# The neighbouring batches' work put inside the second stage's searches, and the next batch's normalisation between the products of the fourth and sixth stage

## Chip, core and metric

The kernel runs on one core of one Trainium2 chip. TensorE (PE) multiplies matrices, VectorE (DVE), ScalarE (ACT) and GpSimd (POOL) work element by element, SyncE (SP) issues the DMAs. The metric is the device time of one execution in microseconds (us).

## The reference

Eight layers run one after the other on x, a residual stream of 4 batches x 512 rows x 512 columns; each begins with a layer norm of x. What matters here are three of them:

```python
# second stage (L0_ffn): 2048 hidden values a row, of which the largest 204 are kept
z = x_flat @ ternary_quant(W_syn).T + b_syn
k = max(1, int(N * (1.0 - TARGET_SPARSITY)))
topv, _ = jax.lax.top_k(z, k)
hidden = jnp.where(z >= topv[:, -1:], jax.nn.relu(z), 0.0)
out = hidden @ ternary_quant(W_out).T + b_out
return layernorm(x + out, gamma, beta)
# fourth stage (L1_ffn)
out = jnp.einsum('bsi,oi->bso', x, weight * scale_weight[:, None]) + bias
# sixth stage (L2_ffn): 8 gates a row, the best one's low-rank update is applied
gate = sigmoid(imp_slope * (score - imp_center)); sel_scale = gate.max(axis=1); sel_idx = gate.argmax(axis=1)
return (1.0 - sel_scale) * x + sel_scale * mod_x_bias
```

## The kernel before, in words

The code writes one program for each engine by hand, and semaphores alone order them; within an engine the order is that of the code. There are eight stages, A to H, and all engines meet at the end of each (`end_stage`). x stays on chip in `X` as 16 tiles of 128 rows. A batch is four tiles. Float32 operands of products are split into a high and a low part (`xT_hi`, `xT_lo`), the high part copied by ScalarE and the low part subtracted by VectorE out of the same PSUM bank.

**Second stage.** Per batch, in a loop: `norm_vector`, `norm_pool`, `norm_tensor` and `norm_scalar` normalise and transpose four tiles; TensorE makes z in `ps` (32 products a tile) and VectorE writes it to `b_z` (L1142). VectorE takes the maximum of each of the four tiles' rows (L1151). Then a search of 26 rounds finds each row's threshold by halving: in a round each tile (here also called a group, 0 to 3) has its values above a candidate counted; groups 0 and 1 are counted by VectorE (`search_vector`, L158), 2 and 3 by ScalarE with a Sign (`search_scalar`, L166), and GpSimd makes the next candidate from each count in the order 2, 0, 3, 1 (`search_pool`, L185 to L190, and L191, which quarters the step once a round). A group's next count waits for its candidate (`search_try`), GpSimd waits for its count (`search_cnt`). After the search VectorE masks z (L1158), TensorE transposes the hidden values (L1784), ScalarE and VectorE split them (L759, L1165), TensorE multiplies by the second matrix (32 products a tile), and VectorE adds the rest, normalises and adds to `X` (L1174 to L1186).

**Fourth stage.** Per batch: normalise four tiles, then for each tile 12 products and one update of `X` (L1281).

**Sixth stage.** Per batch: normalise four tiles, 12 products of 136 columns a tile (L1410 takes them out of PSUM), the gates in some 35 small operations around an exponential on ScalarE, a transposition of the chosen gates, and the output product with its update of `X` (L1450, L1452).

## Time and profile before

| | |
|---|---|
| median of three runs | 3627.24 us (3622.87 to 3627.38) |
| the profiled execution | 3632.95 us |
| its span, first to last instruction | 3631.2 us |
| mean granted TensorE clock | 0.814 of full speed |
| second stage | 159.9 to 1072.1 us of the span |
| fourth stage | 1297.9 to 1404.8 us |
| sixth stage | 2282.2 to 2443.4 us |

The page gives the busy time of each engine. A window gives the same for a stretch of the span, with the granted clock of TensorE (1.00 is 2.4 GHz, 0.50 is 1.2). A group of instructions is one source line on one engine; the idle time in its row is that of its engine just before it, with what ended it. The median and the profiled execution are 5.7 us apart.

### The profile page before, as it was taken

What the parts mean: (1) busy time and instruction counts of PE and PEld (TensorE: products, weight loads), DVE (VectorE), ACT (ScalarE), POOL (GpSimd) and SP (SyncE); (2) the same over time, 40 slices, a digit from 0 to 9 for tenths busy, and PEclk for the clock granted to TensorE, in tenths of its full rate; (3) what the DMA queues carried; (4) which work ended last, traced back from release to release, by engine and by line L of the source; (5) the groups of instructions that cost most, each with busy time, mean ns of one, the idle gap of its engine ahead of it and who ended that gap; (6) DMA issues with size and microseconds to landing.
All of it is one profiled execution on the core that took longest, in us unless ns stands there. A gap on an engine that the chain in (4) does not pass through costs nothing.

```text
span 3631.2 us, 41752 instructions
## 1 busy us (share of the span) xinstructions
PE 2379.0 (66%) x12378; PEld 1982.2 (55%) x12378; DVE 2470.6 (68%) x4232; ACT 1680.2 (46%) x3289; POOL 823.8 (23%) x2434
## 2 busy tenths in 40 slices
PE   3322505226051066699999999456999928999998
PEld 2212404114041055577878788445887827888887
DVE  7888697886979953276767777555777756454443
ACT  3466292561929801255555555114666614333332
POOL 1044161340614500022222222012223320000000
PEclk7665857658575586699999999657999969999999
DMA  4000000000000003644444443003222225332232
GB/s 166 12 0 0 0 0 0 0 0 0 0 13 0 0 18 127 237 138 129 137 129 137 122 146 98 8 12 85 58 56 59 53 76 180 104 111 96 99 111 73
DMA packets 93950, 253.40 MB, mean 70 GB/s; under 512 B 17692, under 2 KB 18972, under 8 KB 86628
## 3 DMA queue, kind: packets, MB, share of 16 engines
q1 hardware_dynamic: 91236, 243.00, 21.5%
q0 software_dynamic: 2560, 8.42, 0.6%
q8 instruction: 87, 1.43, 0.2%
q14 instruction: 67, 0.55, 0.0%
HBM read 162.20 MB, written 22.05 MB: 51 GB/s over the span
## 4 chain that ended last, share of the span: by engine, by line
PE 45%; DVE 11%; issue 9%; ACT 4%; DMA 2%; POOL 1%; SPq 1%; POOLq 0%; ACTq 0%; DVEq 0%; PEldq 0%
PE ps L87 12%; PE ps L89 11%; PE ps L88 11%; PE ps L1905 3%; DVE c_junks L1252 2%; PE ps L2041 1%; ACT c_junks L166 1%; DVE g_pT_lo L1521 1%; PE ps L1895 1%; PE ps L1896 1%; PE ps L1931 1%; PE ps L1934 1%; DVE e_k_lo L1309 1%; DVE e_cT_lo L1387 1%; ACT g_p L927 1%
## 5 line engine op out<-in xcount | busy, mean ns | idle before, releaser
L166 ACT ACTIVATE b_junk_high<-b_z,b_tk 128x2048 bf16<-128x2048 f32 x208 | 414.7, 1994 | 210.3 <-POOLq L172 149.9
L158 DVE TENSOR_SCALAR_CACHE_REDUCE b_junk_low<-b_z,b_tk 128x2048 bf16<-128x2048 f32 x208 | 471.8, 2342 | 1.7 <-POOLq L175 1.7
L1784 PE MATMUL ps<-ident,b_z 128*128 128x128 f32 x256 | 43.3, 341 | 560.1 <-DVEq L1159 533.5
L1784 PEld LDWEIGHTS ps<-ident,b_z 128*128 128x128 f32 x256 | 40.1, 182 | 564.1 <-DVEq L1159 535.2
L604 POOL TENSOR_SCALAR e_p<-e_p,e_st 128x512 f32<-128x512 f32 x256 | 173.6, 698 | 662.4 <-DVE e_st L1329 662.4
L826 ACT ACTIVATE e_p<-ps,e_st 128x512 f32<-128x512 f32 x256 | 173.8, 686 | 144.4 <-DVE e_st L1318 144.4
L1324 DVE TENSOR_TENSOR e_pT_lo<-ps,e_pT_hi 128x512 fp32r<-128x512 f32 x256 | 174.0, 680 | 46.2 <-ACT e_pT_hi L832 42.3
L638 POOL TENSOR_SCALAR g_p<-g_p,g_st 128x128 f32<-128x128 f32 (+3 forms) x256 | 132.2, 537 | 311.7 <-DVE g_st L1502 311.7
L185 POOL TENSOR_SCALAR b_tk<-b_tk 128x1 f32<-128x1 f32 x416 | 122.0, 293 | 299.0 <-DVEq L197 192.4
L927 ACT ACTIVATE g_p<-ps,g_st 128x128 f32<-128x128 f32 (+3 forms) x256 | 131.6, 526 | 80.7 <-DVE g_st L1497 80.7
L1613 DVE TENSOR_TENSOR h_h<-ps,h_sg 128x512 f32<-128x512 f32 (+1 forms) x80 | 50.9, 637 | 173.5 <-ACT h_sg L976 173.3
L1318 DVE TENSOR_REDUCE e_st<-ps 128x1 f32<-128x512 f32 x256 | 163.7, 681 | 2.3 <-PE ps L1896 2.3
L976 ACT ACTIVATE h_sg<-ps 128x512 f32<-128x512 f32 (+1 forms) x80 | 44.3, 553 | 246.0 <-PE ps L89 246.0
L166 ACT ACTIVATE c_junks<-c_sim,c_tk 128x512 bf16<-128x512 f32 x208 | 146.7, 707 | 1.0 <-POOL c_tk L190 1.0
L87 PE MATMUL ps<-xT_hi,h_w_hi 128*128 128x512 f32 (+1 forms) x384 | 139.1, 362 | 9.3 <-issue 6.9
L1521 DVE TENSOR_TENSOR g_pT_lo<-ps,g_pT_hi 128x512 fp32r<-128x512 f32 (+1 forms) x192 | 103.4, 594 | 54.3 <-ACT g_pT_hi L940 54.3
L832 ACT ACTIVATE e_pT_hi<-ps 128x512 fp32r<-128x512 f32 x256 | 138.7, 599 | 3.3 <-PE ps L1905 3.3
L1252 DVE TENSOR_SCALAR_CACHE_REDUCE c_junks<-c_sim,c_tk 128x512 bf16<-128x512 f32 x208 | 140.0, 745 | 0.0
L89 PE MATMUL ps<-xT_hi,h_w_lo 128*128 128x512 f32 (+1 forms) x384 | 137.2, 357 | 0.0
L1905 PE MATMUL ps<-ident,e_p 128*128 128x128 f32 x1024 | 134.3, 275 | 4.2 <-POOL e_p L604 2.3
L88 PE MATMUL ps<-xT_lo,h_w_hi 128*128 128x512 f32 (+1 forms) x384 | 136.7, 356 | 0.0
L1832 PE MATMUL ps<-c_a,ident 128*128 128x128 f32 x128 | 26.6, 292 | 164.1 <-DVE c_a L1212 164.1
(465 smaller groups left out, 8244.0 us busy)
## 6 DMA issues: line engine op xcount, KB each, us to landing
h_w<-in_l_blob SPq DMA_DIRECT2D x80, 512.0 KB, 3.6
e_g<-e_g_kept SPq DMA_DIRECT2D x32, 1024.0 KB, 6.1
e_qkw<-e_qkw_kept SPq DMA_DIRECT2D x32, 640.0 KB, 4.2
h_w<-in_l_blob SPq DMA_DIRECT2D x80, 256.0 KB
e_xs<-e_q_hi SPq DMA_DIRECT2D x128, 128.0 KB, 2.3
e_g_kept<-e_g SPq DMA_DIRECT2D x8, 1024.0 KB, 6.0
e_xs<-e_k_hi SPq DMA_DIRECT2D x64, 128.0 KB, 2.3
e_k<-e_k_hi SPq DMA_DIRECT2D x64, 128.0 KB, 2.3
```

The costliest lines, as they stand in the source:

```text
L87: pe.matmul(o, l_hi, r_hi, start=start, stop=False)
L88: pe.matmul(o, l_hi, r_lo, start=False, stop=False)
L89: return pe.matmul(o, l_lo, r_hi, start=False, stop=stop)
L158: dve.tensor_scalar(junk[j], data[:, j, :], cand[:, j:j + 1], 0.0, ALU.is_ge, ALU.add, accum_out=cnt[:, j:j + 1])\
L166: act.activation(junk[j], data[:, j, :], ACT.Sign, bias=cand[:, j:j + 1], accum_out=cnt[:, j:j + 1])\
L604: pool.tensor_scalar(p, p, e_st[:, h % 2, 8 + t:9 + t], 1.0, ALU.mult, ALU.mult).then_inc(sem("e_scaled"), 1)
L826: act.activation(e_p[:, h % 2, t, :], ps[:, (h * TB + t) % 3, :], ACT.Exp, bias=e_st[:, h % 2, t:t + 1], accum_out=e_st[:, h % 2, 4 + t:5 ...
L927: act.activation(g_p[:, n % 2, G_ROW[t]:G_ROW[t + 1]], ps[:, G_BANK[t], G_COL[t]:G_COL[t] + (t + 1) * P], ACT.Exp, bias=g_st[:, n % 2, t:t ...
L1252: dve.tensor_scalar(c_junk[j], c_sim[:, j, :], cand[:, j:j + 1], 0.0, ALU.is_ge, ALU.add, accum_out=cnt[:, j:j + 1])\
L1318: dve.tensor_reduce(e_st[:, h % 2, t:t + 1], ps[:, (h * TB + t) % 3, :], AX.X, ALU.max, negate=True)\
L1324: dve.tensor_tensor(e_pT_lo[:, c, :], ps[:, 3 + (h * TB + c) % 3, :], e_pT_hi[:, c, :].bitcast(F32), ALU.subtract)\
L1905: t = pe.transpose(ps[:, 3 + n % 3, t_ * P:(t_ + 1) * P], e_p[:, h % 2, t_, c * P:(c + 1) * P], ident[:, :])
```

## The change

In the second stage the loops are written out. While batch i is searched, the rounds are taken in pairs (p = 0 to 12) and the engines do pieces of two other batches between the counts: of batch i+1 the statistics, normalisation, transposes, z and maxima, at the pairs that the tables `B_XN`, `B_LOW`, `B_MADE`, `B_Z` and `B_TOP` name for its four tiles; of batch i-1 the mask, the hidden values' transposes and split, the second product, and the last normalisation. z is held twice (`b_z[:, 2, ...]`); the hidden values go through two 128-column slots of `xT_hi` and `xT_lo`, a quarter of a tile at a time. In odd rounds group 1 is counted by ScalarE instead of VectorE, with the sign turned and GpSimd's comparison with it. The counts' output is int8 instead of bf16. ScalarE normalises x (an Identity with scale and bias) instead of VectorE, and makes the rest for the second residual the same way; the tail has two fused operations where there were three. VectorE loads `b_out` into `xn[:, 3]` and it is waited for at the start. After the last search, batch 3's rest has nothing beside it.

In the fourth stage the 16 tiles go through one software pipeline: tile n's product is issued with tile n+2's transposes ahead of it and tile n+3's normalisation on VectorE, and the first tiles are normalised before the weights are waited for. In the sixth stage the next batch's statistics, normalisation and transposes are put between the gates and the outputs of this one (`f_xn` is held twice), and operations that were issued for each tile are issued once for four.

```diff
+B_XN, B_LOW, B_MADE, B_Z, B_TOP = (2, 4, 7, 8), (4, 6, 8, 9), (4, 7, 8, 9), (6, 8, 9, 10), (7, 10, 11, 11)
 # SyncE
+                sp.dma_start(b_out, inp["b_out"].partition_broadcast(P)).then_inc(sem("b_bsyn_in"), 16)
 # GpSimd, second stage
+                def b_round_pool(i, r):
+                    now, then = (odd, even) if r % 2 else (even, odd)
+                    for g in (2, 0, 3, 1):
+                        q = slice(g, g + 1)
+                        pool.wait_ge(sem(f"search_cnt{g}"), ROUNDS * i + r + 1)
+                        if g == 1 and r % 2:
+                            k(pool.tensor_scalar(take[:, q], cnt[:, q], float(HID - 2 * SYN_K), now[:, q], ALU.is_le, ALU.mult))
+                        else:
+                            enough = float(SYN_K if g < 2 else 2 * SYN_K - HID)
+                            k(pool.tensor_scalar(take[:, q], cnt[:, q], enough, now[:, q], ALU.is_ge, ALU.mult))
+                        k(pool.tensor_tensor(low[:, q], low[:, q], take[:, q], ALU.add))
+                        pool.tensor_tensor(cand[:, q], low[:, q], then[:, q], ALU.add).then_inc(sem(f"search_try{g}"), 1)
 # ScalarE, second stage
+                def b_hidden_scalar(i, j, q):
+                    n = (i * TB + j) * 4 + q
+                    act.wait_ge(sem("b_hT_ps"), n + 1)
+                    if n >= 2:
+                        act.wait_ge(sem("b_hT_used"), n - 1)
+                    act.activation(xT_hi[:, :, (2 + q % 2) * P:(3 + q % 2) * P], ps[:, q % 2, :].rearrange("p (c t) -> p c t", c=4), ACT.Copy)\
+                        .then_inc(sem("b_hT_hi"), 1)
+                def b_count_scalar(i, r, g):
+                    act.wait_ge(sem(f"search_try{g}"), search_tries(i, r))
+                    act.activation(b_junk[:, g, :], b_z[:, i % 2, g, :], ACT.Sign, bias=cand[:, g:g + 1], scale=-1.0 if g == 1 else 1.0,
+                                   accum_out=cnt[:, g:g + 1]).then_inc(sem(f"search_cnt{g}"), 1)
+                for i in range(B):
+                    for p in range(ROUNDS // 2):
+                        b_count_scalar(i, 2 * p, 2)
+                        b_count_scalar(i, 2 * p, 3)
+                        if i and p < 2 * TB:
+                            for q in range(2):
+                                b_hidden_scalar(i - 1, p // 2, p % 2 * 2 + q)
+                        if i and p in (2, 4, 6, 8):
+                            b_rest_scalar(i - 1, (p - 2) // 2)
+                        if i + 1 < B:
+                            for t in range(TB):
+                                if p == B_XN[t]:
+                                    b_xn_scalar(i + 1, t)
+                                if p == B_LOW[t]:
+                                    b_turned_scalar(i + 1, t)
+                        b_count_scalar(i, 2 * p + 1, 2)
+                        b_count_scalar(i, 2 * p + 1, 3)
+                        b_count_scalar(i, 2 * p + 1, 1)
 # VectorE, second stage
+                for i in range(B):
+                    for p in range(ROUNDS // 2):
+                        b_count_vector(i, 2 * p, 0)
+                        b_count_vector(i, 2 * p, 1)
+                        b_count_vector(i, 2 * p + 1, 0)
+                        if i:
+                            if p in (2, 4, 6, 8):
+                                b_sum_vector(i - 1, (p - 2) // 2)
+                            if p < 2 * TB:
+                                for q in range(2):
+                                    b_hidden_vector(i - 1, p // 2, p % 2 * 2 + q)
+                            if p in (1, 3, 5):
+                                b_mask_vector(i - 1, (p + 1) // 2)
+                            if p in (3, 5, 7, 9):
+                                b_tail_vector(i - 1, (p - 3) // 2)
...
+                    b_end_vector(i)
+                    if i + 1 < B:
+                        b_begin_vector(i + 1)
+                    b_mask_vector(i, 0)
 # TensorE, second stage
+                for i in range(B):
+                    for p in range(ROUNDS // 2):
+                        if i and p < 2 * TB:
+                            for q in range(2):
+                                b_hidden_tensor(i - 1, p // 2, p % 2 * 2 + q)
+                        if i + 1 < B:
+                            for t in range(TB):
+                                if p == B_LOW[t]:
+                                    b_turn_tensor(i + 1, t)
+                        if i and p < 2 * TB:
+                            for q in range(2):
+                                b_out_tensor(i - 1, p // 2, p % 2 * 2 + q)
+                        if i + 1 < B:
+                            for t in range(TB):
+                                if p == B_MADE[t]:
+                                    b_z_tensor(i + 1, t)
 # VectorE, fourth stage
+                for n in range(TILES):
+                    i, j = divmod(n, TB)
+                    if n + 3 < TILES:
+                        xn_vector("d", (n + 3) // TB, (n + 3) % TB)
+                    if j == 0 and i + 1 < B:
+                        dve.wait_ge(sem("ln_xn"), TB * (ln_turn("d", i) + 1))
+                        d_norm_vector(i + 1)
+                    k.later(dve.tensor_tensor(X[:, n, :], X[:, n, :], d_rows[:, 1, :], ALU.add))
+                    if n + 2 < TILES:
+                        d_turned_vector(n + 2)
+                    dve.wait_ge(sem("y_ps"), n + 1)
 # TensorE, sixth stage
+                for i in range(B):
+                    pe.wait_ge(sem("f_m"), i + 1)
...
+                    for u in range(2):
+                        if i + 1 < B:
+                            f_turn_tensor(i + 1, 2 * u)
+                            f_turn_tensor(i + 1, 2 * u + 1)
+                        f_y_tensor(i, 2 * u)
+                        f_y_tensor(i, 2 * u + 1)
+                    if i + 1 < B:
+                        for j in range(TB):
+                            f_a_tensor(i + 1, j)
```

Here is VectorE inside a search before: the loop body with both its counts (b_junk_low is the count's output, b_z the values, b_tk the candidates and counts).

```order
L1151 TENSOR_REDUCE b_tk<-b_z 128x1
L37 REGISTER_ALU
L1152 MEMSET b_tk 128x2
L1153 TENSOR_SCALAR b_tk<-b_tk 128x2
L37 REGISTER_ALU
L195 TENSOR_SCALAR b_tk<-b_tk 128x2
L196 TENSOR_TENSOR b_tk<-b_tk 128x2
L37 REGISTER_ALU
L154 UNCONDITIONAL_BRANCH
L154 ISA
L158 TENSOR_SCALAR b_junk_low,b_tk<-b_z,b_tk 128x2048 x2
L154 REGISTER_ALU
```

And VectorE in the second search of the changed kernel, pairs 5 and 6 (L1273 is the count, L1289 the hidden values' low part, L1284 the mask, L1305 to L1308 a tail, L1296 to L1301 a sum).

```order
L1273 TENSOR_SCALAR b_junk,b_tk<-b_z,b_tk 128x2048 x3
L1289 TENSOR_TENSOR xT_lo<-ps,xT_hi 128x4x128 x2
L1284 SCALAR_TENSOR_TENSOR b_z<-b_z,b_edge 128x2048
L1305 SCALAR_TENSOR_TENSOR xn<-xn,b_st,b_rows 128x512
L1307 SCALAR_TENSOR_TENSOR xn<-xn,b_st,b_rows 128x512
L1308 TENSOR_TENSOR X_rows<-X_rows,xn 128x512
L1273 TENSOR_SCALAR b_junk,b_tk<-b_z,b_tk 128x2048 x3
L1296 SCALAR_TENSOR_TENSOR xn<-ps,b_st,xn 128x512
L1298 TENSOR_TENSOR xn<-xn 128x512
L1299 BN_STATS b_st<-xn 128x6
L1300 BN_AGGR b_st<-b_st 128x2
L1301 TENSOR_SCALAR b_st<-b_st 128x1
```

Three counts a pair are left where there were four, and behind them stand the pieces of the neighbouring batches.

ScalarE before: a loop of two counts a round (L166), and the hidden values' copies (L759) behind the whole search.

```order
L162 ISA
L166 ACTIVATE b_junk_high,b_tk<-b_z,b_tk 128x2048 x2
L162 REGISTER_ALU
L162 COMPARE_AND_BRANCH
L758 ISA
L759 ACTIVATE b_hT_hi<-ps 128x512
L758 REGISTER_ALU
L759 ACTIVATE b_hT_hi<-ps 128x512
```

ScalarE in the second search of the changed kernel, pairs 1 to 4 (L814 is the count, L802 the hidden values' high part, L809 the rest, L789 the normalisation, L794 the normalised tile's high part).

```order
L814 ACTIVATE b_junk,b_tk<-b_z,b_tk 128x2048 x5
L802 ACTIVATE xT_hi<-ps 128x4x128 x2
L814 ACTIVATE b_junk,b_tk<-b_z,b_tk 128x2048 x5
L802 ACTIVATE xT_hi<-ps 128x4x128 x2
L809 ACTIVATE xn<-X_rows,b_ln 128x512
L789 ACTIVATE xn<-X_rows,b_ln 128x512
L814 ACTIVATE b_junk,b_tk<-b_z,b_tk 128x2048 x5
L802 ACTIVATE xT_hi<-ps 128x4x128 x2
L814 ACTIVATE b_junk,b_tk<-b_z,b_tk 128x2048 x5
L802 ACTIVATE xT_hi<-ps 128x4x128 x2
L809 ACTIVATE xn<-X_rows,b_ln 128x512
L794 ACTIVATE xT_hi<-ps 128x4x128
```

Five counts stand between two groups of pieces, where a search had four a pair and nothing between them.

## Rows read from the trace of the kernel before

**Rows 1.** The page's busy time of each engine, share of the span and instructions.

```profile
PE 2379.0 (66%) x12378; PEld 1982.2 (55%) x12378; DVE 2470.6 (68%) x4232; ACT 1680.2 (46%) x3289; POOL 823.8 (23%) x2434
```

**Rows 2.** Windows: length, busy us of each engine, clock, DMA share, GB/s.

```profile
206.90:331.70 124.80, 0.00 (x0) 0.00 (x0) 122.99 (x111) 106.20 (x104) 75.50 (x338) 0.50 0.00 0
331.70:388.10 56.40, 41.15 (x192) 34.55 (x192) 40.11 (x57) 8.92 (x16) 2.23 (x5) 0.80 0.00 0
...
159.90:1072.10 912.20, 299.00 (x1344) 246.84 (x1344) 751.63 (x825) 469.66 (x496) 315.01 (x1372) 0.66 0.00 1
...
1297.90:1404.80 106.90, 63.15 (x256) 50.94 (x256) 57.84 (x107) 11.37 (x17) 4.07 (x4) 0.79 0.04 15
...
2282.20:2443.40 161.20, 80.55 (x328) 67.66 (x328) 92.22 (x269) 25.11 (x58) 4.04 (x4) 0.54 0.02 5
```

**Rows 3.** Groups by line: count, busy us, mean ns, idle before.

```profile
L158 DVE TENSOR_SCALAR_CACHE_REDUCE b_junk_low<-b_z,b_tk 128x2048 bf16<-128x2048 f32 x208 | 471.8, 2342 | 1.7 <-POOLq L175 1.7
L166 ACT ACTIVATE b_junk_high<-b_z,b_tk 128x2048 bf16<-128x2048 f32 x208 | 414.7, 1994 | 210.3 <-POOLq L172 149.9 <-POOL b_tk L190 56.1
...
L1142 DVE SCALAR_TENSOR_TENSOR b_z<-ps,b_st,b_bsyn 128x512 f32<-128x512 f32 x64 | 48.1, 751 | 77.8 <-PE ps L1774 77.8
...
L1158 DVE SCALAR_TENSOR_TENSOR b_z<-b_z,b_tk 128x2048 f32<-128x2048 f32 x16 | 37.6, 2352 | 1.9 <-DVE b_z L1158 0.6
...
L1151 DVE TENSOR_REDUCE b_tk<-b_z 128x1 f32<-128x2048 f32 x16 | 36.6, 2286 | 1.0 <-DVE b_tk L196 0.5
...
L1165 DVE TENSOR_TENSOR xT_lo<-ps,xT_hi 128x512 fp32r<-128x512 f32 x32 | 20.8, 687 | 9.4 <-ACT xT_hi L759 9.2
...
L759 ACT ACTIVATE xT_hi<-ps 128x512 fp32r<-128x512 f32 x32 | 17.8, 601 | 59.8 <-PE ps L1784 59.8
```

**Rows 4.** Timeline of the first search's start: start, us, instruction.

```profile
212.49 2.35 DVE L158 TENSOR_SCALAR_CACHE_REDUCE b_junk_low<-b_z,b_tk 128x2048 bf16<-128x2048 f32 x1 [0.43 <-POOLq L175]
...
214.76 2.34 DVE L158 TENSOR_SCALAR_CACHE_REDUCE b_junk_low<-b_z,b_tk 128x2048 bf16<-128x2048 f32 x1
215.06 0.29 POOL L185 TENSOR_SCALAR b_tk<-b_tk 128x1 f32<-128x1 f32 x1 [1.43 <-DVE b_junk_low L158]
...
216.00 0.29 POOL L185 TENSOR_SCALAR b_tk<-b_tk 128x1 f32<-128x1 f32 x1
...
216.86 2.00 ACT L166 ACTIVATE b_junk_high<-b_z,b_tk 128x2048 bf16<-128x2048 f32 x1 [1.10 <-POOL b_tk L190]
```

**Rows 5.** Timeline of TensorE, second product of the first batch.

```profile
348.77 0.63 PE L1797 MATMUL ps<-b_tout,b_hT_hi 128*128 128x512 f32 x1
349.20 0.63 PE L1798 MATMUL ps<-b_tout,b_hT_lo 128*128 128x512 f32 x1
```

**Rows 6.** Windows around the end of TensorE's work in batch 0.

```profile
382.00:384.00 2.00, 0.00 (x0) 0.00 (x0) 1.93 (x3) 0.00 (x0) 0.00 (x0) 0.97 0.00 0
384.00:394.00 10.00, 0.36 (x2) 0.36 (x3) 7.12 (x19) 0.00 (x0) 1.57 (x2) 0.50 0.00 0
```

**Rows 7.** Timeline of VectorE, a tile's sum and statistics.

```profile
374.53 0.75 DVE L1174 SCALAR_TENSOR_TENSOR b_y<-ps,b_st,xn 128x512 f32<-128x512 f32 x1 [0.38 <-PE ps L1798]
...
377.11 0.15 DVE L1181 TENSOR_SCALAR b_st<-b_st 128x1 f32<-128x1 f32 x1
```

**Rows 8.** Timeline of VectorE, fourth stage.

```profile
1311.35 2.46 DVE L111 BATCH_NORM_STATS2 ln_stats<-X_rows 128x6 f32 x4
...
1324.31 0.75 DVE L1281 SCALAR_TENSOR_TENSOR X_rows<-ps,tg,X_rows 128x512 f32 x1 [2.50 <-PE ps L89]
...
1327.11 0.75 DVE L1281 SCALAR_TENSOR_TENSOR X_rows<-ps,tg,X_rows 128x512 f32 x1 [1.45 <-PE ps L89]
```

**Rows 9.** Timeline of VectorE, sixth stage.

```profile
2294.27 2.48 DVE L111 BATCH_NORM_STATS2 ln_stats<-X_rows 128x6 f32 x4 [0.24 <-DVE f_const L1402]
...
2313.23 0.29 DVE L1410 TENSOR_TENSOR f_a<-ps,f_const 128x128 f32<-128x128 f32 x1 [2.07 <-PE ps L89]
...
2331.39 2.47 DVE L111 BATCH_NORM_STATS2 ln_stats<-X_rows 128x6 f32 x4 [0.56 <-DVE X_rows L1452]
```

More of the change, by code:

```diff
@@ L23, with b_bank @@
 B_PIECES = 4
+B_XN, B_LOW, B_MADE, B_Z, B_TOP = (2, 4, 7, 8), (4, 6, 8, 9), (4, 7, 8, 9), (6, 8, 9, 10), (7, 10, 11, 11)
+def b_bank(n):
+    return 4 if n >= TILES - TB and n % 2 else 2
 BANK = 512
@@ L563, in _ @@
             if stages > 1:
[L564 to L571 removed]
+                low, even, odd, cand, cnt, take = (b_tk[:, q, :] for q in range(6))
@@ new lines, in _ @@
+                b_ln_pool(0)
+                for i in range(B):
+                    b_begin_pool(i)
+                    for r in range(ROUNDS):
+                        b_round_pool(i, r)
+                        p = r // 2
+                        if r % 2 == 0:
+                            if p == 1 and i + 1 < B:
+                                b_ln_pool(i + 1)
+                            if i and p in (3, 5, 7, 9):
+                                b_row_pool((i - 1) * TB + (p - 3) // 2)
@@ L761, in _ @@
+                for j in range(TB):
+                    for q in range(4):
+                        b_hidden_scalar(B - 1, j, q)
+                    b_rest_scalar(B - 1, j)
                 end_stage(act, 1)
@@ new lines, in b_end_vector, with b_mask_vector @@
+                def b_end_vector(i):
+                    for g in range(4):
+                        dve.wait_ge(sem(f"search_try{g}"), search_tries(i, ROUNDS))
+                    k.later(dve.tensor_scalar(b_edge[:, 2:4], low[:, 2:4], -1.0, None, ALU.mult))
+                    k(dve.tensor_copy(b_edge[:, 0:2], low[:, 0:2]))
+                def b_mask_vector(i, j):
+                    z = b_z[:, i % 2, j, :]
+                    dve.scalar_tensor_tensor(z, z, b_edge[:, j:j + 1], z, ALU.is_ge, ALU.mult).then_inc(sem("b_h"), 1)
@@ L1801, in _ @@
+                for q in range(2):
+                    b_hidden_tensor(B - 1, 0, q)
+                for n in range(4 * TB):
+                    b_out_tensor(B - 1, n // 4, n % 4)
+                    if n + 2 < 4 * TB:
+                        b_hidden_tensor(B - 1, (n + 2) // 4, (n + 2) % 4)
                 end_stage(pe, 1)
```

544 lines of the change are left out of this document (332 added, 212 removed).

## The prediction

> **What bounds the kernel now.** I read the page's busy shares first: no engine is busy throughout (VectorE 68%, TensorE 66%) [rows 1], so a single engine's sum says nothing and each stage has to be read alone. The windows by stage come next: the second stage takes 912.2 us, a quarter of the span, with TensorE busy 299.0 us in it; the fourth takes 106.9, the sixth 161.2 [rows 2]. Inside the second stage one batch has a search of 124.8 us with TensorE at nothing and VectorE full, then 56.4 us of masking, transposing and the second product, and then normalisation and first product [rows 2]. The batch repeats every 228 us (912.2/4). So two phases alternate, and in each the engine of the other one idles. In the search VectorE is the bound: two counts a round, issued 2.27 us apart [rows 4], make 4.54 us a round, 118 in 26 rounds; ScalarE needs 2 x 1.994 = 4.0 [rows 3].
>
> **The second stage.** The change puts everything else of a batch inside another batch's search and moves one count in four from VectorE to ScalarE. I work in pairs of rounds, as the new code does, p = 0 to 12. A pair costs VectorE 3 x 2.27 = 6.8 us plus what stands behind its counts, and ScalarE 5 x 2.0 = 10.0 plus what stands between its. A count begun at 212.49 is taken up by GpSimd at 215.06, 2.57 later; its three steps for a group repeat after 0.94 (215.06 to 216.00), and the count that they release begins 0.86 after they do (216.00 to 216.86) [rows 4]. GpSimd takes the groups in the order 2, 0, 3, 1: 4 x 0.94 and some 0.4 for the quartering make 4.2 us a round and 8.4 a pair, so it doesn't bound. An empty pair is therefore ScalarE's 10.0: a bare search becomes 13 x 10.0 = 130 us against 119 now. That is the cost of the change.
>
> The work put in, from rows: a low part of hidden values 0.65 (two make 1.3), mask 2.35, a row of z 0.76 (four make 3.1), maximum 2.3, ScalarE's copy 0.6 [rows 3]; sum and statistics of a tile 2.75, from 374.53 to the end at 377.26 [rows 7]; the tail three of the 0.69 to 0.75 kinds, 2.3; statistics of a batch 3.2, the four of 2.46 together [rows 8] and 0.7 for their aggregation. ScalarE's new normalisation and rest are Identity operations over 512 columns, for which no row stands; bounds are the 0.6 of the copy and half the 2048-wide count, 1.0; I take 0.7. The int8 output of the counts has no row either; bf16 and f32 outputs of 2048 columns cost VectorE 2.34 and 2.35 [rows 3], so nothing is taken, with the open end priced below.
>
> For a middle batch the VectorE extras over p = 0 to 12 are 4.5, 3.9, 4.1, 6.0, 4.8, 6.0, 7.9, 5.9, 6.6, 6.1, 5.4, 4.6, 0 (sum 65.8), ScalarE's 1.2, 1.2, 2.6, 1.2, 3.2, 1.2, 2.5, 1.9, 2.0, 0.6, 0, 0, 0 (17.6). By engine sums: VectorE 88.5 + 65.8 = 154, ScalarE 148. Neither can run freely: ScalarE's second group-3 count of a pair waits until VectorE's first count of the pair is through GpSimd and group 3 behind it, 2.57 + 0.94 + 0.94 = 4.45 us after that count began, and VectorE's group-1 count waits for ScalarE's last one of the pair before. So a pair lasts about the longer of both.
>
> TensorE adds waits. At the half clock its 512-column products are 0.43 us apart [rows 5], at the full one 2.80/12 = 0.23 [rows 8]. It enters each burst cold: two us after its last product the clock has fallen to 0.50 [rows 6]. Sixteen products of a pair's two quarters thus take some 5.8 us (between 3.7 warm and 6.9 cold). For p = 4, 7, 8 and 9 a z tile of 32 follows in the same queue, 7.5 us warm, 13.7 cold. TensorE's work of pair 4 begins when VectorE has passed its counts, the sum and the first low part, 10.4 us in; 5.8 and 7.5 later it is free, and only then come pair 5's transposes, for which ScalarE stands waiting, with two hidden copies and then three counts queued behind. That is 7 us lost; the turn at p = 8, behind z at p = 7, loses about 2.
>
> Walking the pairs with these numbers, the lengths are 11.3, 10.7, 12.5, 12.8, 11.7, 19.1, 14.7, 12.7, 14.3, 12.9, 12.3, 11.4, and 13.8 for the last with the end of one search, the start of the next and mask 0 ahead of VectorE's first count: 170 us. The first batch has only the next batch's work, 139 (near 10.5 a pair); the last only the previous batch's, 149. Ahead of the searches stand 47 us, as now to ScalarE's first count (159.9 to 206.9): VectorE's maxima go between the z tiles, which gives its counts an earlier start, but ScalarE, now the bound of batch 0, doesn't start earlier. Behind the last search is nothing to hide in: four tiles at about 15 us each (6 of TensorE, ScalarE and VectorE taking turns over the four quarters, 7.5 of mask, sum and tail, and rest waiting for the tail before it), with the first mask 69 us, against 56 now [rows 2]. Sum 47 + 139 + 2 x 170 + 149 + 69 = 744 against 912: **-168**.
>
> **The fourth stage.** The stage begins at 1297.9 [rows 2]; its weights are ready at 1311.4, then normalisation runs, and the first output comes at 1324.3 [rows 8]. Now the first three tiles are normalised while the weights are on their way, so the first product starts at 1311.5, cold, and its output comes near 1317.4 . After that TensorE needs 2.8 + 0.5 for four transposes, 3.3 a tile; VectorE 0.68 + 0.69 + 0.69 + 0.75 = 2.8, and 3.2 more once a batch, 3.6 on average. Fifteen tiles make 53; end at 1371 instead of 1404.8 [rows 2]: **-33**.
>
> **The sixth stage.** A batch takes 37.1 us now (2294.27 to 2331.39), 18.2 of them from the last product's output to the next batch; before a tile's product VectorE idles 2.07, and its own two operations make it 2.56 a tile, 10.2 for four [rows 9]. In the new order the chain of a batch is: gating before the exponential 3.3 (from the last product on eighteen small operations become nine, 1.5 less), the next batch's statistics 3.2, gating after it 2.2 (0.6 less), the next batch's normalisation with the transposed gates' copy behind it 2.4, their low part 0.7, then turns and outputs sharing TensorE 7.2, and the next four products 10.2. Period 29.2, three times 7.8 less than now; the last batch is shorter by 3; the start is earlier by 6.5, since the first normalisation fits into the weights' loading although it makes the weights' low parts 3 us late. In all **-33**. The other stages have no edit that costs time.
>
> **Sum.** The profiled execution took 3632.95 (span 3631.2): 3632.95 - 168 - 33 - 33 = 3399. It lay 5.7 above the median of the runs, 3627.24, which is small against what is open; I give 3398. A measurement of this kernel tells 0.2%, some 7 us, from no change.
>
> **Rivals.** (a) The clock stays at half for everything in the searches. For it speaks the fall to 0.50 within four us of the last product [rows 6], and that bursts of 9 us stand in pairs of 12; against it that bursts are dense. The stall at p = 5 grows by 8, those at p = 8 to 10 by 14: 22 a middle batch, and 16 at the end: +60, 3458. The Trainium skill, TensorE: Matmul & The Clock Gate, section on HAM oscillation, speaks for this rival: products issued in bursts with idle gaps between them lose the full clock each time, so spreading them out is what it warns of. The trace agrees that gaps lower the clock; whether the bursts win it back is open.
> (b) TensorE keeps the full clock from pair to pair: bursts 3.7, stall at p = 5 halved. -4 to -5 a middle batch, -7 at the end: 3383.
> (c) The hand-overs serialise: both engines' extras add up in each pair instead of overlapping (middle batch 130 + 66 + 18 = 214, first and last less). +130: 3530. Against it: the waits in the code are for earlier rounds.
> (d) Slower: the int8 output makes ScalarE's counts dearer. ScalarE has 5 of a pair, 260 in all; the 234 us of gain are gone when each costs 0.9 more, 2.9 instead of 2.0. At 3.0 the time is 3659. Nothing in the rows speaks for it; the output's type made 0.01 between bf16 and f32 on VectorE.
>
> **How the numbers follow.** My forecast has 0.72, with a range of its own of 3370 to 3430 (5 us a batch of the second stage and 5 each for its end and the two other stages, nearly all to one side); (a) 0.15, (b) 0.07, (c) 0.04, (d) 0.02. Leaving out (c), (d) and the far side of the forecast's spread, the range is 3370 to 3460. Faster 0.97, same 0.01, slower 0.02.
>
> **What would show it.** Batches of the second stage end about 139, 170, 170 and 149 us apart; ScalarE 85% busy or more there and its count still 2.0; a pair without extras 10.0. Pair 5 of batches 1 and 2 the longest, with ScalarE waiting for transposes. The stage's length 744, the fourth 73, the sixth 128. I am wrong if a count is longer than 2.05, if GpSimd's round passes 5 us, or if the middle batches exceed 185, which would be (a) or (c): (a) if TensorE's products are 0.43 apart throughout, (c) if they are not.

## Result and profile after

The changed kernel takes 3371.89 us (median of four runs, 3368.83 to 3372.44) against 3627.31 of the kernel before beside it: ratio 0.929, 95% interval 0.9268 to 0.9312. The forecast was 3398 with a range from 3370: it is 26 us faster than the forecast, 2 us inside the end of the range. The profiled execution has a span of 3370.2, 261.0 less than the 3631.2 of before.

The page's busy shares, as in [rows 1], first:

```profile
PE 2406.1 (71%) x12378; PEld 1991.6 (59%) x12378; DVE 2313.4 (69%) x4028; ACT 1792.3 (53%) x3425; POOL 848.4 (25%) x2430
```

VectorE has 157 us less work (52 counts went to ScalarE, and fewer small operations remain), ScalarE 112 more. Windows by stage, in the columns of [rows 2]: the second, the fourth and the sixth stage; batch 1 of the second stage; and what stands behind its last search.

```profile
159.90:897.50 737.60, 340.55 (x1344) 267.48 (x1344) 613.00 (x697) 583.04 (x632) 341.06 (x1368) 0.73 0.01 2
1122.00:1191.50 69.50, 56.33 (x256) 45.00 (x256) 55.42 (x107) 11.49 (x17) 5.17 (x4) 0.88 0.07 23
2063.20:2181.60 118.40, 76.56 (x328) 65.87 (x328) 76.06 (x193) 25.02 (x58) 4.04 (x4) 0.57 0.02 6
345.03:511.69 166.66, 85.96 (x336) 67.75 (x336) 151.68 (x174) 145.51 (x159) 87.29 (x342) 0.77 0.00 0
825.40:897.50 72.10, 44.85 (x192) 35.02 (x192) 38.22 (x54) 12.34 (x22) 4.64 (x7) 0.83 0.00 0
```

Against [rows 2] the second stage is 174.6 shorter (forecast 168), the fourth 37.4 (33), the sixth 42.8 (33). Of the stages without an edit the third is 1.3 shorter, the fifth 5.7 shorter (871.7 for 877.4) and the last two 0.8 longer (1188.6 for 1187.8). That makes the 261.0.

The counts, by groups of lines (columns of [rows 3]):

```profile
L814 ACT ACTIVATE b_junk<-b_z,b_tk 128x2048 int8<-128x2048 f32 x260 | 516.6, 1993 | 28.7 <-POOLq L574 25.2
L1273 DVE TENSOR_SCALAR_CACHE_REDUCE b_junk<-b_z,b_tk 128x2048 int8<-128x2048 f32 x156 | 360.5, 2342 | 42.4 <-POOL b_tk L590 41.7
```

The int8 output costs nothing: 1993 and 2342 ns, to the nanosecond almost what [rows 3] has for bf16. The search has the shape that the prediction drew: ScalarE waits only 28.7 us before its 260 counts.

ScalarE's timeline shows the lengths. A batch begins with the first row of its searches, and pair 5 of batch 1 lies between 405.88 and 424.74:

```profile
205.53 2.00 ACT L814 ACTIVATE b_junk<-b_z,b_tk 128x2048 int8<-128x2048 f32 x1 [18.02 <-POOLq L574]
215.47 1.98 ACT L814 ACTIVATE b_junk<-b_z,b_tk 128x2048 int8<-128x2048 f32 x1
...
345.03 2.00 ACT L814 ACTIVATE b_junk<-b_z,b_tk 128x2048 int8<-128x2048 f32 x1 [2.40 <-POOLq L574]
...
405.88 2.00 ACT L814 ACTIVATE b_junk<-b_z,b_tk 128x2048 int8<-128x2048 f32 x1
...
417.81 1.08 ACT L802 ACTIVATE xT_hi<-ps 128x512 fp32r<-128x512 f32 x2 [7.85 <-PE ps L2015]
...
424.74 1.99 ACT L814 ACTIVATE b_junk<-b_z,b_tk 128x2048 int8<-128x2048 f32 x1
...
459.38 0.60 ACT L794 ACTIVATE xT_hi<-ps 128x512 fp32r<-128x512 f32 x1 [5.83 <-PE ps L1993]
...
511.69 2.00 ACT L814 ACTIVATE b_junk<-b_z,b_tk 128x2048 int8<-128x2048 f32 x1 [2.40 <-POOLq L574]
...
678.85 2.00 ACT L814 ACTIVATE b_junk<-b_z,b_tk 128x2048 int8<-128x2048 f32 x1 [2.40 <-POOLq L574]
```

The first pair, without extras, is 9.94 (205.53 to 215.47). Batches are 139.5, 166.7, 167.2 and 146.6 long (the last search's counts end at 825.4). In pair 5 ScalarE idles 7.85 us for TensorE's transposes, in pair 8 another 5.83. TensorE in pair 4 and 5, second product, z and transposes:

```profile
404.62 0.63 PE L2026 MATMUL ps<-b_tout,xT_lo 128*128 128x512 f32 x1
405.05 0.63 PE L2026 MATMUL ps<-b_tout,xT_hi 128*128 128x512 f32 x1
...
408.54 0.40 PE L2026 MATMUL ps<-b_tout,xT_lo 128*128 128x512 f32 x1
408.77 0.39 PE L2026 MATMUL ps<-b_tout,xT_hi 128*128 128x512 f32 x1
...
417.17 1.03 PE L2015 MATMUL ps<-ident,b_z 128*128 128x128 f32 x8
```

This burst starts at 0.43 us a product and is at 0.23 from the tenth on; the sixteen from 404.03 to 409.7 take 5.7 us. Between them and the transposes at 417.17 stand the 32 products of z, 7.5 us.

The fourth stage on VectorE has its first output at 1142.14, the next 3.24 later, the sixteenth at 1190.80:

```profile
1142.14 0.75 DVE L1480 SCALAR_TENSOR_TENSOR X_rows<-ps,tg,X_rows 128x512 f32<-128x512 f32 x1 [1.55 <-PE ps L94]
1145.38 0.75 DVE L1480 SCALAR_TENSOR_TENSOR X_rows<-ps,tg,X_rows 128x512 f32<-128x512 f32 x1 [0.83 <-PE ps L94]
...
1190.80 0.75 DVE L1480 SCALAR_TENSOR_TENSOR X_rows<-ps,tg,X_rows 128x512 f32<-128x512 f32 x1 [1.45 <-PE ps L94]
```

Behind the third batch's statistics VectorE has two tiles to catch up and waits for nothing; there a tile costs it 2.3 us:

```profile
1157.30 0.74 DVE L1480 SCALAR_TENSOR_TENSOR X_rows<-ps,tg,X_rows 128x512 f32<-128x512 f32 x1
...
1159.62 0.74 DVE L1480 SCALAR_TENSOR_TENSOR X_rows<-ps,tg,X_rows 128x512 f32<-128x512 f32 x1
```

In the sixth stage VectorE's second read of the gating products marks each batch. The batches repeat after 28.28, 21.36 and 28.30 us:

```profile
2089.05 0.42 DVE L1617 TENSOR_TENSOR f_a<-ps,f_const 128x256 f32<-128x256 f32 x1 [4.55 <-PE ps L94]
...
2117.33 0.42 DVE L1617 TENSOR_TENSOR f_a<-ps,f_const 128x256 f32<-128x256 f32 x1 [4.61 <-PE ps L94]
...
2138.69 0.42 DVE L1617 TENSOR_TENSOR f_a<-ps,f_const 128x256 f32<-128x256 f32 x1 [2.17 <-PE ps L94]
...
2166.99 0.42 DVE L1617 TENSOR_TENSOR f_a<-ps,f_const 128x256 f32<-128x256 f32 x1 [4.62 <-PE ps L94]
```

The windows there go with this: the granted clock is at half up to the second batch's outputs, then full, then half again. That the clock is the cause is tested below (f_paced).

```profile
2104.00:2108.00 4.00, 4.00 (x15) 3.42 (x13) 3.37 (x7) 3.35 (x10) 0.00 (x0) 0.50 0.01 4
...
2129.00:2132.00 3.00, 1.94 (x13) 1.53 (x12) 3.00 (x6) 0.61 (x2) 0.00 (x0) 1.00 0.00 0
...
2148.00:2151.00 3.00, 3.00 (x11) 2.31 (x10) 2.53 (x5) 1.26 (x3) 0.00 (x0) 0.50 0.00 0
```

### The profile page after: what moved, and what is told of

It is laid out like the page before. It is cut to its first block, busy times and chain, and to the rows that moved or that the text cites. A ratio compares the mean times of both kernels' runs of the same rounds, so it can differ in the third digit from the quotient of the medians.

```text
span 3370.2 us, 38781 instructions
## 1 busy us (share of the span) xinstructions
PE 2406.1 (71%) x12378; PEld 1991.6 (59%) x12378; DVE 2313.4 (69%) x4028; ACT 1792.3 (53%) x3425; POOL 848.4 (25%) x2430
## 4 chain that ended last, share of the span: by engine, by line
PE 56%; DVE 24%; ACT 11%; issue 3%; POOL 3%; DMA 2%; SPq 1%; POOLq 0%; ACTq 0%; DVEq 0%; PEldq 0%
PE ps L92 14%; PE ps L94 13%; PE ps L93 13%; ACT b_junk L814 5%; DVE b_junk L1273 4%; PE ps L2170 3%; DVE c_junks L1431 3%; PE ps L2026 2%; PE ps L2005 2%; PE ps L2330 2%; ACT c_junks L163 1%; DVE g_pT_lo L1743 1%; PE ps L2160 1%; PE ps L2161 1%; DVE ln_stats L1113 1%
## 5 line engine op out<-in xcount | busy, mean ns | idle before, releaser
L814 ACT ACTIVATE b_junk<-b_z,b_tk 128x2048 int8<-128x2048 f32 x260 | 516.6, 1993 | 28.7 <-POOLq L574 25.2
L1273 DVE TENSOR_SCALAR_CACHE_REDUCE b_junk<-b_z,b_tk 128x2048 int8<-128x2048 f32 x156 | 360.5, 2342 | 42.4 <-POOL b_tk L590 41.7
L2026 PE MATMUL ps<-b_tout,xT_hi 128*128 128x512 f32 x256 | 128.4, 502 | 139.1 <-DVE xT_lo L1289 139.1
L2026 PEld LDWEIGHTS ps<-b_tout,xT_hi 128*128 128x128 f32 x256 | 62.5, 244 | 160.6 <-DVE xT_lo L1289 146.2
L2005 PE MATMUL ps<-b_tsyn,xT_hi 128*128 128x512 f32 x256 | 110.3, 431 | 61.0 <-DVE b_z L1254 39.5
```

The costliest lines, as they stand in the source:

```text
L814: act.activation(b_junk[:, g, :], b_z[:, i % 2, g, :], ACT.Sign, bias=cand[:, g:g + 1], scale=-1.0 if g == 1 else 1.0, accum_out=cnt[:, g: ...
L1273: dve.tensor_scalar(b_junk[:, g, :], b_z[:, i % 2, g, :], cand[:, g:g + 1], 0.0, ALU.is_ge, ALU.add, accum_out=cnt[:, g:g + 1])\
L2005: u = pe.matmul(ps[:, 4 + q, :], part[:, c, x], b_tsyn[:, c, q * BANK:(q + 1) * BANK], start=(c == 0 and part is xT_hi), stop=(c == C - 1 ...
L2026: u = pe.matmul(ps[:, b_bank(n), :], part[:, c, x], b_tout[:, 4 * q + c, :], start=(q == 0 and c == 0 and part is xT_hi), stop=(q == 3 and ...
```

## The experiments

**The stages one by one.** Three kernels, each with some stages in the new and the others in the old order.

```diff
 b_alone:  second stage new; fourth and sixth as before
 d_alone:  fourth stage new; all others as before
 f_alone:  sixth stage new; all others as before
```

> The changed kernel with its fourth and sixth stage as before: what the second stage is worth by itself. In the changed kernel's profiled execution that stage was 737.6 us long against 912.2, 174.6 less, and the third, unedited, was 1.3 shorter. Theory (the stages' gains add up): 3627 - 176 = 3451, ratio 0.951, fourth and sixth stage 106.9 and 161.2 as before, fifth 877.4 as before. Rival (the later stages take something back or bring something by the state in which they are entered): the fourth to sixth stage differ from before by several us and the total lies outside 3446 to 3456.

> The kernel before with the fourth stage alone in its new order. In the changed kernel the fourth stage was 37.4 us shorter, and the unedited fifth, behind it, 5.7 shorter, all of it in its first 31 us, where TensorE's granted clock came back to full some 10 us earlier than before. Theory (the fifth stage's gain is a consequence of how the fourth one hands over to it): 37.4 + 5.7 = 43, 3584, ratio 0.988, with the clock at 0.9 behind the fifth stage's first products. Rival (the clock's return there has nothing to do with the fourth stage): the fifth stage stays 877 long, gain 37, 3590, ratio 0.990.

> The kernel before with the sixth stage alone in its new order. In the changed kernel its batches repeated after 28.3, 21.4 and 28.3 us: in the second the product's tiles took 1.34 us each at the full clock, in the others 2.5 at half. My forecast had 29.2 for all. Theory (the new order's own price is 28.3 a batch, and a full clock in one of them is a matter of where that batch falls): a gain between 35 (all at half) and 43 (one at full), 3584 to 3592, with the warm batch in another place or missing. Rival (the order itself brings the second batch to full speed each time): the periods 28.3, 21.4, 28.3 again, gain 43, 3584, ratio 0.988.

Measured beside a kernel before of 3632.22: 3456.99 (0.9518, interval 0.9503 to 0.9533), 3596.06 (0.9900, 0.9885 to 0.9915) and 3594.21 (0.9893, 0.9878 to 0.9908). In us 175, 36 and 38, together 249, where the whole change gave 255 and in a second measurement (below) 260; each interval is some 5 us to either side, so the stages' gains add up within the noise. b_alone's total lies 1 us outside the rival's 3446 to 3456, but the kernel before was 5 us slower beside it than the 3627 of the sum, and the gain of 175 is the theory's 176. The second stage was 737.15 long again, with batches of 139.4, 166.5, 167.2 and 146.6: its length is the code's and hardly moves. The windows of the fourth and fifth stage of b_alone and of d_alone, and of the fourth of f_alone (old, new and old order in the fourth):

```profile
1123.20:1232.25 109.05, 64.89 (x256) 52.08 (x256) 57.87 (x106) 11.47 (x17) 4.06 (x4) 0.77 0.04 15
1232.25:2105.05 872.80, 800.98 (x4272) 657.03 (x4272) 562.25 (x980) 426.08 (x1009) 195.11 (x277) 0.94 0.47 146
```

```profile
1295.50:1363.35 67.85, 55.07 (x256) 44.16 (x256) 55.53 (x107) 11.50 (x17) 5.18 (x4) 0.90 0.07 24
1363.35:2237.15 873.80, 806.26 (x4272) 661.40 (x4272) 562.66 (x980) 426.84 (x1009) 196.09 (x277) 0.93 0.47 145
```

```profile
1300.80:1412.75 111.95, 68.30 (x256) 54.70 (x256) 57.91 (x107) 11.46 (x17) 4.06 (x4) 0.74 0.04 14
```

The theory that the new fourth stage hands a full clock to the fifth fell. The fifth is 872.8 behind an old fourth stage and 873.8 behind a new one, and in d_alone the clock is at 0.50 in the second ten us of it. The old fourth stage, too, was 106.9, 109.05 and 111.95 long in three profiles, with a clock of 0.79, 0.77 and 0.74. So a stage can differ by 5 us from one profile to the next without any edit. The new order's 67.85 in d_alone, against 69.5 in the changed kernel, is such a difference too.

The sixth stage in f_alone was 114.6 long, 46.6 less than before, while the whole kernel gained 38: in the same profile the fourth stage was 5 longer and the stages behind the sixth 3.7. Its periods were 28.30, 21.54 and 28.29: the second batch was the warm one (at full clock) again. So here my "matter of where that batch falls" was wrong; in all eight profiles with this stage as the change has it the three periods were 28.3, 21.4 to 21.6 and 28.3. What differs is its start: the first mark comes 25.8 us into the stage in three of the profiles and 21.8 in five. This is the clock as well, in the first batch's 136-column gating products. In the changed kernel they ran at 0.50 throughout; in after_again (below), whose stage is 114.5 long, the clock rose in the middle of them:

```profile
2084.00:2085.00 1.00, 1.00 (x7) 1.00 (x6) 0.30 (x1) 0.00 (x0) 0.00 (x0) 0.50 0.00 0
...
2086.00:2087.00 1.00, 1.00 (x11) 1.00 (x11) 0.00 (x0) 0.00 (x0) 0.00 (x0) 1.00 0.00 0
```

**TensorE's order in the searches** (b_order).

```diff
-    hidden transposes(p); turn(p); second product(p); z(p)
+    second product(p); hidden transposes(p+1); turn(p+1); z(p)     # where p has a z tile
```

> The changed kernel with one thing moved in TensorE's order in the second stage: the transposes of the next pair are issued ahead of the current pair's tile of z and no longer behind it. Nothing else is touched. In the changed kernel ScalarE stands idle 7.85 us in pair 5 and 5.83 in pair 8 of batches 1 and 2, for transposes that stand behind 32 products of z. Theory (TensorE's queue is the cause of both): both waits go, a middle batch falls from 166.7 to about 153, the first from 139.5 to about 137, in all some 30 us: 3342, ratio to the kernel before 0.921. Rival 1 (VectorE takes over: it was busy 151.7 of the 166.7): middle batches 158 to 162, total 3352 to 3362. Rival 2 (the waits move behind another step, the mask or a low part): total within 7 us of 3372.

Measured: 3352.05, ratio 0.9222 (0.9209 to 0.9234), 20 us less than the changed kernel. ScalarE in pair 4 to 5, and batch 1 as a window:

```profile
406.82 2.00 ACT L814 ACTIVATE b_junk<-b_z,b_tk 128x2048 int8<-128x2048 f32 x1
410.20 1.09 ACT L802 ACTIVATE xT_hi<-ps 128x512 fp32r<-128x512 f32 x2 [1.30 <-PE ps L2015]
```

```profile
343.84:501.92 158.08, 87.24 (x336) 68.46 (x336) 151.34 (x174) 146.10 (x159) 90.73 (x342) 0.77 0.00 1
```

The wait of 7.85 is 1.30, and pair 8 fell from 17.8 to 11.8. TensorE's queue was the cause of both. But the batch gained 8.6 and not the 13.7 of the two waits: pairs 10 and 11 grew from 9.9 and 10.1 to 12.1 and 11.6, since VectorE, busy 151.3 of 158.1, is now the one to wait for. That is rival 1, at the low end of its batches and of its total; the theory's 3342 was missed by 10.

**One count in four** (v_fourth), all of groups 0 and 1 on VectorE.

```diff
-    ScalarE: count(2p+1, group 1)
+    VectorE: count(2p+1, group 1)
```

> The changed kernel with VectorE taking every count of groups 0 and 1, as before the change, so that ScalarE has four counts of a pair and VectorE four. It tells what moving one count in four is worth. Theory (a pair lasts as long as the busier engine): VectorE's busy time in a middle batch rises from 151.7 by 13 counts of 2.27 to 181, and the batch from 166.7 to 182 to 187; the first batch from 139.5 to some 149, the last from 146.6 to some 156. Together +50 to +60: 3425, ratio 0.944. A bare pair becomes 9.1. Rival (the hand-overs through GpSimd set the length and not the sums): the batches grow by under 5 each, total under 3390.

Measured: 3432.90, ratio 0.9449 (0.9430 to 0.9468). The second stage is 799.2 instead of 737.6, with batches of 145.7, 188.5, 188.0 and 154.9; VectorE is busy 180.63 of the 188.54 of batch 1:

```profile
351.13:539.67 188.54, 87.15 (x336) 68.48 (x336) 180.63 (x200) 121.34 (x133) 91.03 (x342) 0.74 0.00 0
```

The batch is a little above the 182 to 187 expected, and far from the rival's 5 us: the busier engine sets the length, as in the walk through the pairs. Of the second stage's 174.6 us this one count brings 61.6.

**That count only where VectorE has other work** (b_split), on top of b_order.

```diff
+    VectorE takes count(2p+1, group 1) where p is in {0: (1, 2, 3, 5, 12), 1: (11, 12), 2: (11, 12), 3: (8, 9, 10, 11, 12)}[batch]
```

> The kernel with TensorE's transposes ahead of z, and with the fourth count given to VectorE again in those pairs in which it has no other work: p = 1, 2, 3, 5 and 12 of batch 0, 11 and 12 of batches 1 and 2, 8 to 12 of batch 3. Theory (a bare pair is ScalarE's five counts of 1.99, 9.94, and would be VectorE's four of 2.27, 9.1): 0.8 less in each of 14 pairs, 10 to 12 us in all, 3341, ratio to the kernel before 0.919. Rival (a bare pair with four counts each is held by the hand-over from engine to engine and not by the counts): within 3 us of 3352, ratio 0.922.

Measured: 3349.85, ratio 0.9226 (0.9209 to 0.9242), the same as b_order, so the theory's 3341 was missed; the second stage 716.95 against 717.4. In batch 0 the theory held: pairs 1, 2, 3 took 8.4, 8.7 and 8.4 instead of 9.9, 10.6 and 9.9, and the batch 130.7 instead of 137.3. In batch 3 ScalarE's counts ended after 142.9 instead of 145.7, but VectorE's own last count now ends later, and the mask that follows the search begins 147.1 us after the batch's first count in both (657.11 to 804.21, in b_order 660.25 to 807.33): nothing was gained there. And batches 1 and 2 grew by 2.6 and 3.0. The expectation took their pairs 11 and 12 for bare, which they aren't: `B_TOP` puts two maxima, 4.6 us, into pair 11, and VectorE must end the search, start the next and mask before the next batch's first count. Pair 11 fell from 11.6 to 10.1 and pair 12 rose from 13.7 to 17.8.

**The idle stretch of the sixth stage** (f_fill, f_paced).

```diff
 for each batch on TensorE, behind its gating products:
+    f_fill:  16 products of 512 columns into a free bank
+    f_paced: 8; wait for f_z; 8; wait for ln_var; 6     # if another batch follows
     wait for f_m, transpose the gates
```

> The changed kernel with sixteen products of 512 columns, whose results nothing reads, put into the sixth stage on TensorE between a batch's gating products and the transposes of its gates, where it stands idle for some 7.6 us. In the changed kernel the periods were 28.3, 21.4 and 28.3. Theory (the clock makes the difference, and work in the idle stretch keeps or brings it to full): 21.4 to 23 in all three, the stage 118.4 less 10 to 14, in all 3358 to 3362, ratio 0.926. Rival 1 (the order of the work makes the difference and not the clock, or the clock stays at half in spite of the work): 28.3, 21.4, 28.3 again, 3372. Rival 2 (sixteen cold products are 6.9 us and reach past the moment at which the gates are ready): the cold batches grow by about a microsecond. The Trainium skill, TensorE: Matmul & The Clock Gate, section on HAM oscillation, holds that idle gaps between bursts are what loses the full clock: by that rule the theory holds.

> The changed kernel with the idle stretch of TensorE in the sixth stage filled in three pieces, of 8, 8 and 6 products of 512 columns, the second and third let go by VectorE's own progress. Sixteen in one piece ended 4 us before the gates were ready in the first batch, at full clock, and the clock was at 0.50 when the transposes came; in the second and third batch it stayed full. Theory (a gap of 4 us is what lost it): periods of about 21.3 for all three, the stage 100 to 104 against 118.4 and 106.9 with sixteen in one piece, 3355 to 3358, ratio 0.925. Rival (the first batch can't be warm, whatever stands in the gap): 28.3, 21.3, 21.3 again, 107.

f_fill: 3364.75, ratio 0.9266 (0.9247 to 0.9284), the stage 106.9 long (with the early start of 21.8, so 7.6 us come from the filler); periods 28.28, 21.26, 21.27. The third period fell to 21.3, the first did not. TensorE there, and the windows:

```profile
2088.80 3.87 PE L2265 MATMUL ps<-xT_hi 128*128 128x512 f32 x16
2096.67 1.07 PE L2268 MATMUL ps<-ident,f_m 128*72 128x128 f32 x4 [4.00 <-DVE f_m L1645]
```

```profile
2089.00:2092.00 3.00, 3.00 (x14) 2.46 (x14) 2.72 (x10) 0.23 (x1) 0.00 (x0) 1.00 0.00 0
2092.00:2095.00 3.00, 0.67 (x3) 0.21 (x2) 2.90 (x11) 0.00 (x0) 0.35 (x1) 0.94 0.00 0
2095.00:2098.00 3.00, 1.33 (x6) 0.91 (x7) 2.72 (x12) 0.23 (x1) 0.65 (x1) 0.50 0.02 5
```

At full clock the sixteen last 3.87 us; 4.00 idle ones follow and the clock is at 0.50. In the third batch it did not stay full either, as the next expectation has it: behind 4.02 idle us it was at 0.50 from 2146 to 2149, but then it came back, and the period was 21.27 all the same. Why it came back there and not in the first batch is open. f_paced spreads the products: 3359.74, ratio 0.9245 (0.9231 to 0.9260), periods 21.27, 21.28 and 21.27.

```profile
2064.75:2169.05 104.30, 74.47 (x394) 60.93 (x394) 75.63 (x193) 24.70 (x58) 4.04 (x4) 0.83 0.03 8
2084.00:2090.00 6.00, 6.00 (x30) 6.00 (x29) 0.51 (x2) 0.00 (x0) 0.00 (x0) 0.50 0.00 0
2090.00:2096.00 6.00, 5.50 (x19) 4.17 (x18) 5.07 (x18) 0.23 (x1) 0.00 (x0) 0.74 0.00 0
2096.00:2102.00 6.00, 4.20 (x21) 2.94 (x22) 5.69 (x18) 1.68 (x3) 1.01 (x1) 1.00 0.01 3
```

The stage is 104.3 against 118.4 with the same start of 25.8: 7 us for each of the two batches that were cold (at half clock). TensorE does 66 more products and the stage gets shorter. The clock, and nothing in the order, made 28.3 out of 21.3. The Trainium skill, TensorE: Matmul & The Clock Gate, section on HAM oscillation, holds that gaps between bursts lose the full clock. f_fill agrees with it twice, with 0.50 behind 4.00 and 4.02 idle us; in `best`, below, the clock falls without such a gap.

That the gap of 4 us was what f_fill's first batch lost by is not shown, since f_paced differs in more: it entered its first filler at 0.50, and the clock rose in it, at 2093.

**The fifth stage's start** (e_fill): 36 products of 512 columns while TensorE waits for the first weights.

```diff
 TensorE, start of the fifth stage:
+    36 products of 512 columns into a free bank
     first weights' products
```

> The changed kernel with 36 products of 512 columns, whose results nothing reads, on TensorE at the start of the fifth stage, where it waits 10.4 us for the first weights. The fifth stage, which the change doesn't edit, was 877.5 us long before and 871.7, 872.8, 873.8, 875.1 and 874.2 in the five profiles behind it, with the clock in its first 40 us at another level each time. Theory (that spread is the clock's state at the stage's first products): with the clock held at full from its start the stage is 868 to 871 long, ratio 0.928. Rival (the weights' arrival sets the first stretch and the clock follows from it): 871 to 876, within 4 us of 3372.

Measured: 3370.43, ratio 0.9279 (0.9264 to 0.9295), the stage 870.2 long. The clock was held at full for ten us and was gone ten us later:

```profile
1190.85:1200.85 10.00, 8.46 (x36) 6.68 (x36) 4.95 (x13) 0.00 (x0) 4.16 (x5) 1.00 0.91 347
1200.85:1210.85 10.00, 6.05 (x32) 4.76 (x32) 1.47 (x4) 2.28 (x7) 2.59 (x2) 0.84 0.24 98
1210.85:1220.85 10.00, 8.64 (x27) 6.39 (x28) 1.88 (x4) 1.32 (x4) 0.00 (x0) 0.50 0.84 321
```

The 870.2 lies in the theory's 868 to 871, but it is only 1.5 below the shortest of the other profiles (871.7 to 877.4), and the total can't be told from the changed kernel's. What sets this stage's spread stays open.

**The end of the second stage** (b_end).

```diff
 VectorE behind the last search, tile j, quarter q:
     low part(j, q)
-    behind all four quarters: mask(j+1); sum(j-1); tail(j-1)
+    j == 0 and q > 0: mask(q);   j > 0 and q == 1: sum(j-1);   j > 0 and q == 2: tail(j-1)
```

> The changed kernel with VectorE's order alone changed behind the last search: the last three masks go between the quarters of the first tile and no longer one behind each tile's quarters, and a tile's sum and tail go behind the second and third quarter of the next. I put this end at 69 us as four tiles of 15, with the engines taking turns, and it was 72.1. Theory (what lengthens it is that the next tile's transposes wait for a mask, and ScalarE's rest for a tail, while VectorE stands idle between quarters): 11 to 12 us a tile, the stage shorter by 16 to 24, 3350 to 3356, ratio 0.924. Rival (TensorE's own cold products and turns make the 15): under 5 us less.

Measured: 3349.50, ratio 0.9216 (0.9202 to 0.9230).

```profile
823.41:875.10 51.69, 40.92 (x192) 32.18 (x192) 37.72 (x54) 12.61 (x21) 3.33 (x7) 0.90 0.00 0
```

51.7 instead of 72.1: 20.4 us from the order of one engine's operations, none added or removed. TensorE's 192 operations went from 44.85 busy us to 40.92 as the clock rose from 0.83 to 0.90.

**The changed kernel again, and all that helped.**

> The changed kernel once more, unedited, beside the three below. The stages that no experiment touched came out differently from one profile to the next (the fifth 870.2 to 876.5, the start of the sixth 21.7 or 25.8). Theory (that is the clock's state from execution to execution, the same for every kernel): 3372 within 4, ratio 0.929, with stages of 737, 118 or 114 and 870 to 877. Rival (something of a kernel's own sets them): the very stages of the first profile again, 737.6, 69.5, 871.7 and 118.4.

Measured: 3372.45, ratio 0.9282 (0.9270 to 0.9295); stages 737.3, 69.55, 875.3 and 114.5, periods 28.28, 21.54 and 28.29. The second stage and the fourth repeat; the fifth is 3.6 longer and the sixth 3.9 shorter, nearly all of it in its start. The theory held.

```diff
+    best: b_order, b_end and f_paced together, and the b_split rule with {0: (1, 2, 3, 5), 3: (8, 9, 10, 11, 12)}
```

> All that helped in one kernel: the transposes ahead of z, the end of the second stage in the new order, the sixth stage's gap filled in three pieces, and VectorE's fourth count only in batch 0 (p = 1, 2, 3, 5) and batch 3 (p = 8 to 12), where pairs fell from 9.9 to 8.4 and 9.1. Theory (the parts add up): 3352 less 8 less 18 less 14, 3312, ratio 0.912. Rival (the end's and the gap's gains fail or overlap): 3325 to 3345, ratio 0.916 to 0.921.

Measured: 3310.18 (3305.61 to 3327.40), ratio 0.9121 (0.9097 to 0.9144), 62 us less than the changed kernel beside it and within 2 of the theory. The second stage and the sixth:

```profile
159.55:845.50 685.95, 328.26 (x1344) 257.93 (x1344) 629.32 (x716) 567.89 (x614) 349.59 (x1368) 0.75 0.01 2
...
2014.95:2121.94 106.99, 75.90 (x394) 61.97 (x394) 75.70 (x193) 24.70 (x58) 4.04 (x4) 0.80 0.03 7
```

The second stage is 51.4 us shorter than in the changed kernel beside it, most of it from the two reorderings and from batch 0 (130.3; in b_order 137.3); batch 3's counts on VectorE brought nothing in b_split, and no run shows them alone. The middle batches are 157.0, the end 51.8. The sixth came out at 107 and not 100: its third period was 27.67, so the pacing doesn't hold the clock in every execution.

## Why the prediction came out as it did

The forecast for the profiled execution, 3399, was 27 us too slow: 6.6 in the second stage, 4.4 in the fourth, 9.8 in the sixth and 6.2 in stages without an edit. The overlap of the batches came as forecast. What failed were terms of the sum: above all the sixth stage's "Period 29.2, three times", then the fourth stage's "3.6 on average".

**Second stage, right in mechanism and nearly in size.** Term by term, forecast and measured: ahead of the searches 47 and 45.6, first batch 139 and 139.5, middle batches 170 and 166.7 and 167.2, last 149 and 146.6, end 69 and 72.1; in all 744 and 737.6. An empty pair is 9.94 (10.0). The pairs of batch 1 were 11.5, 12.6, 12.3, 11.8, 12.8, 18.9, 12.1, 12.0, 17.8, 11.4, 9.9, 10.1 and 13.7. Pair 5, at 19.1 in the forecast, is 18.9, with ScalarE waiting for the transposes behind z; b_order shows that this queue is the cause. Mis-sized were the wait at pair 8 (5.8 for "about 2") and, the other way, pair 6 (12.1 for 14.7) and pairs 9 to 11 (31.4 for 36.6): I had VectorE come late into them. But while ScalarE stood in pairs 5 and 8, VectorE caught up, and ScalarE's bare 9.9 ruled; with those waits gone, in b_order, pairs 10 and 11 are 12.1 and 11.6, near the 12.3 and 11.4 that I had. The end of 69 was worked out from the turns that engines take, and these came (72.1); b_end shows that the turns were not needed.

**Fourth stage, -33 forecast, -37.4 in the profile and -36 by itself.** The step that failed is VectorE's "2.8, and 3.2 more once a batch, 3.6 on average". The first output came 20.1 us into the stage (19.5). Fifteen tiles then took 48.7, 3.24 each, and not 53, and 3.24 is TensorE's pace, which the sum had as 3.3. The 2.8 added up the durations in the rows, but where VectorE waits for nothing a tile takes 2.3 (1157.30 to 1159.62), since each operation starts before the duration of the one ahead is over (one of 0.68 at 1158.42, the next at 1159.02); and only two of the batches' statistics, 3.0 each, fall behind the first output. That is 15 x 2.3 + 2 x 3.0, or 41 us for fifteen tiles, 2.7 each and below TensorE's. TensorE was a tile ahead, so the statistics delayed nothing for long. VectorE waited 0.83 a tile for it, wherever it wasn't catching up.

**Sixth stage, -33 forecast, -42.8 in the profile and -38 by itself, the largest miss.** The step that failed is "Period 29.2, three times". The two cold periods were 28.3, 0.9 under it, and the second was 21.4, since the clock was at full there. Start and end together took 40.5 us, as in the sum (128 less 87.6), but that is luck in part: in five of the eight profiles the start is 4 us shorter by the clock. In the search I weighed the clock, with two rivals for it; in this stage I took it at the half speed of [rows 2] as given, though a denser order can change exactly that. f_paced shows the size: 7.0 us a batch.

**The other stages.** "No edit that costs time" was right, but some 6 of the 26 us came, in the profiled execution, from stages with none (1.3 and 5.7 less, 0.8 more). They spread by as much between profiles without an edit, so this part is no effect of the change.

**Rivals.** (a) and (b), the clock at half or at full throughout the searches: neither. The prediction's "It enters each burst cold" holds for most bursts, not for all. In batch 1 those behind 4.6 to 10.4 idle us (355.46, 379.66, 404.03, 434.90, 446.13) began at 0.43 us a product and were at 0.23 after six to eleven; two behind 1.73 and 0.97 (388.31, 419.18) ran at 0.23 almost from their start. The one in front of the long wait took 5.7 us for sixteen products where I took 5.8. (c): middle batches of 167, not 214. (d): 1993 ns a count. ScalarE was busy 87% of a middle batch. The range's 28 us below the point were the sizes of the single terms, added as if nearly all went to one side. 26 of them were used up: all three stages came out faster than forecast, and the stages without an edit, for which the range had nothing, another 6 in the profile. That the time still lies 2 us inside the range is luck.

## What to carry to other kernels

Filling one engine's idle phase with another batch's work pays until the two engines' sums in a unit of the pipeline are equal; walk through it in units, with each engine's instructions in order, and look in every queue for work that another engine waits for, standing behind work that nobody waits for. Two such reorderings were worth 20 us each here (b_order, b_end), with nothing added or taken away. Don't take a pair for bare before looking up what its tables put into it, and measure a search's end by the last engine that counts in it (b_split). A denser order can also change TensorE's clock, so a stage's old spacing is only one of two bounds for its new one, and the other belongs in the range.
